# LSTM step with attention in a decoder: the first part's sum of exponentials on VectorE, the first alpha copy on ScalarE

## The reference

```python
def attend(h):
    q = h @ Wq.T
    scores = jnp.einsum('bc,bsc->bs', q, context)
    alpha = jax.nn.softmax(scores, axis=-1)
    ctx = jnp.einsum('bs,bsc->bc', alpha, context)
    return jnp.tanh(jnp.concatenate([ctx, h], axis=-1) @ Wout.T + b_out)

def step(carry, x_t):
    h, c, attn = carry
    gates = concat([x_t, attn]) @ W_ih.T + b_ih + h @ W_hh.T + b_hh
    i, f, g, o = jnp.split(gates, 4, axis=-1)
    c = sigmoid(f) * c + sigmoid(i) * tanh(g)
    h = sigmoid(o) * tanh(c)
    out = attn_out = attend(h)
    return ((h, c, attn_out), out)
```

## Time and profile before

| | us |
|---|---|
| median of 3 runs | 5888.53 (5887.12 to 5888.95) |
| profiled execution, its time | 5886.25 |
| profiled execution, its span | 5884.4 |
| PE busy in the span | 5294.2 (90%) |
| DVE busy | 3447.6 (59%) |
| ACT busy | 1998.7 (34%) |
| POOL busy | 352.6 (6%) |

### The profile page before, as it was taken

The page is one execution under the profiler, slowest core; times in us unless marked ns, Lnnn a source line. Parts: engine busy times, 40 slices in busy tenths (PEclk is TensorE's granted clock), DMA queues, the critical chain, the costliest instruction groups (busy, mean ns, idle before and its releaser), DMA issues. The chain is left out here.

```text
span 5884.4 us, 383798 instructions
## 1 busy us (share of the span) xinstructions
PE 5294.2 (90%) x171160; PEld 3829.2 (65%) x171160; DVE 3447.6 (59%) x15922; ACT 1998.7 (34%) x7989; POOL 352.6 (6%) x811
## 2 busy tenths in 40 slices
PE   6899999999999999999999999998887879797989
PEld 2477777777777777777777777776634334444433
DVE  4355555555555555555555555554588999999931
ACT  3143334333433333343334343433212122223221
POOL 0000000000000000000000000000111111112100
PEclk8999999999999999999999999999888889898999
DMA  1100000000000000000000000001211101010111
GB/s 71 59 2 2 2 2 2 2 2 2 2 2 2 2 2 2 2 2 2 2 2 2 2 2 2 2 2 42 79 45 40 42 24 50 29 50 29 50 39 54
DMA packets 45131, 111.57 MB, mean 19 GB/s; under 512 B 8160, under 2 KB 10208, under 8 KB 44528
## 3 DMA queue, kind: packets, MB, share of 16 engines
q1 hardware_dynamic: 43600, 109.39, 6.1%
q10 hardware_dynamic: 1440, 1.06, 0.1%
HBM read 99.90 MB, written 10.52 MB: 19 GB/s over the span
## 5 line engine op out<-in xcount | busy, mean ns | idle before, releaser
L712 PE MATMUL lstm_part_ps<-lstm_keys,lstm_hid 128*4 128x128 f32 x32768 | 1024.3, 273 | 205.7 <-DVE lstm_hid L881 205.7
L728 PE MATMUL lstm_ctx_ps<-lstm_values,lstm_alpha 128*4 128x128 f32 (+1 forms) x49152 | 1051.0, 237 | 0.0
L712 PEld LDWEIGHTS lstm_part_ps<-lstm_keys,lstm_hid 128*4 128x4 f32 x32768 | 770.2, 86 | 429.2 <-DVE lstm_hid L881 414.9
L728 PEld LDWEIGHTS lstm_ctx_ps<-lstm_values,lstm_alpha 128*4 128x4 f32 x49152 | 902.7, 86 | 91.5
L910 DVE TENSOR_REDUCE lstm_neg_max<-lstm_part_ps 128x1 f32<-128x128 f32 x1024 | 299.0, 292 | 678.1 <-PE lstm_part_ps L712 678.1
L844 ACT ACTIVATE lstm_expo<-lstm_part_ps,lstm_neg_max 128x128 f32<-128x128 f32 x1024 | 376.9, 368 | 861.6 <-DVE lstm_neg_max L910 861.6
L863 DVE STREAM_TRANSPOSE lstm_gates<-lstm_half_ps 128x96 f32<-128x96 f32 x1026 | 290.0, 283 | 597.7 <-PE lstm_half_ps L671 573.6
L671 PE MATMUL lstm_half_ps<-lstm_w_hid,lstm_hid 128*13 128x96 f32 x16384 | 600.8, 245 | 0.0
L671 PE MATMUL lstm_half_ps<-lstm_w_attn,lstm_attn 128*13 128x96 f32 x16448 | 447.9, 246 | 0.0
L671 PEld LDWEIGHTS lstm_half_ps<-lstm_w_hid,lstm_hid 128*13 128x13 f32 x16384 | 379.8, 93 | 0.0
L1944 ACT ACTIVATE mix_gated<-mix_gate_ps 115x512 f32<-115x512 f32 (+2 forms) x200 | 112.6, 563 | 774.9 <-PE mix_gate_ps L1672 774.8
(11 more groups left out here) (325 smaller groups left out, 8378.6 us busy)
## 6 DMA issues: line engine op xcount, KB each, us to landing
mix_ring<-in_sm_chunks SPq DMA_DIRECT2D x120, 358.0 KB, 3.0
mix_ring<-in_mix_chunks SPq DMA_DIRECT2D x80, 384.0 KB, 3.1
lstm_xg<-xg_rows SPq DMA_DIRECT2D x514, 16.0 KB
xg_rows<-lstm_xg_tile SPq DMA_DIRECT2D x16, 512.0 KB, 2.6
ctxT<-in_ctxT SPq DMA_DIRECT2D x1, 2048.0 KB, 14.3
out_xT<-xT SPq DMA_DIRECT2D x4, 512.0 KB, 3.8
xT<-in_xT SPq DMA_DIRECT2D x1, 1536.0 KB, 9.3
lstm_w_x<-in_lstm_w_x SPq DMA_DIRECT2D x1, 1024.0 KB, 10.3
```

What stands on the lines that cost most here:

```text
L712: mm = pe.matmul(part_rows(score_ps[part], b), hid[:, k, lo:lo + SPACE], keys[:, k, b * SRC + c * P:b * SRC + (c + 1) * P], start=(n == 0 ...
L728: mm = pe.matmul(part_rows(ctx_ps[n], b), alpha[:, b, c, SPACE - 1 - c:2 * SPACE - 1 - c], values[:, b * SC + c, ctx_cols[n]], start=(c == ...
```

## The change

It does three things in the LSTM step. The first part's exponential no longer has an accumulator: `exp_ready` is now raised by the exponential itself, and VectorE sums `expo[:, 0, :]` with a reduction of its own, raising the new `first_total_ready`. ScalarE instead of VectorE copies the first turned part to `alpha`, between its two exponentials. The second exponential keeps its accumulator. VectorE's copy of alpha 1 moves ahead of the spread of the totals. `alpha_ready` becomes one semaphore for each part.

```diff
@@ tensor
-                        pe.wait_ge(alpha_ready, 2 * t + 1)
+                        pe.wait_ge(alpha_ready[0], t + 1)
                         for n in range(PIECES):
                             context(0, n)
                         pe.wait_ge(exp_ready, 2 * t + 2)
                         turn(1)
                         for n in range(PIECES):
                             context(1, n)
-                        pe.wait_ge(alpha_ready, 2 * t + 2)
+                        pe.wait_ge(alpha_ready[1], t + 1)
@@ scalar
                         for part in range(PARTS):
                             act.wait_ge(max_ready, 2 * t + part + 1)
                             act.activation(expo[:, part, :], score_ps[part], ACT.Exp, bias=neg_max[:, part:part + 1],
-                                           accum_out=total[:, part:part + 1]).then_inc(exp_ready, 1)
+                                           accum_out=total[:, 1:PARTS] if part == 1 else None).then_inc(exp_ready, 1)
+                            if part == 0:
+                                act.wait_ge(alpha_turned, 2 * t + 1)
+                                act.copy(alpha_rows(0), turned_rows(0)).then_inc(alpha_ready[0], 1)
@@ vector
-                        keep_turned(t, 0)
                         dve.wait_ge(max_ready, 2 * t + 2)
                         dve.transpose(spread_blocks(spread_max[:, :]), every_row(neg_max[:, :])).then_inc(max_spread, 1)
                         dve.wait_ge(max_spread, t + 1)
                         dve.tensor_reduce(neg_max_all[:, :], spread_values(spread_max[:, :]), AX_XY, ALU.min)\
                            .then_inc(max_all_ready, 1)
+                        dve.wait_ge(exp_ready, 2 * t + 1)
+                        dve.tensor_reduce(total[:, 0:1], expo[:, 0, :], AX_X, ALU.add).then_inc(first_total_ready, 1)
+                        dve.wait_ge(alpha_turned, 2 * t + 2)
+                        dve.tensor_copy(alpha_rows(1), turned_rows(1)).then_inc(alpha_ready[1], 1)
+                        dve.wait_ge(first_total_ready, t + 1)
                         dve.wait_ge(exp_ready, 2 * t + 2)
                         dve.transpose(spread_blocks(spread_total[:, :]), every_row(total[:, :])).then_inc(total_spread, 1)
-                        keep_turned(t, 1)
                         dve.wait_ge(shrink_ready, t + 1)
```

More of the change, by code:

```diff
@@ L612, in attention_lstm_phase @@
             shrink_ready = q.sem("lstm_shrink_ready")
+            first_total_ready = q.sem("lstm_first_total_ready")
             total_spread = q.sem("lstm_total_spread")
@@ L619, in attention_lstm_phase @@
             alpha_turned = q.sem("lstm_alpha_turned")
-            alpha_ready = q.sem("lstm_alpha_ready")
+            alpha_ready = [q.sem(f"lstm_alpha{part}_ready") for part in range(PARTS)]
             ctx_ready = [q.sem(f"lstm_ctx{n}_ready") for n in range(PIECES)]
@@ L644, in by_part, with alpha_rows, turned_rows @@
                 return ap.rearrange("p (a c) -> p a c", a=PARTS)
+            def alpha_rows(part):
+                return alpha[:, :, 2 * part:2 * part + 2, SPACE - 1]
+            def turned_rows(part):
+                return turned_ps[part].rearrange("p (b r) -> p b r", r=2)
             @block.sync
@@ L882, in new_hidden @@
                                              in1=tanh_c[:, k, :], op0=ALU.add, op1=ALU.mult).then_inc(h_ready[k], 1)
[L884 to L887, removed]
                 for ps in (*half_ps, *part_ps, *ctx_bank):
```

## The result

| | before | after |
|---|---|---|
| median | 5888.53 us | 5857.91 us (5 runs, 5854.18 to 5859.06) |
| ratio | | 0.9947, 95% interval 0.9933 to 0.9960 |
| profiled span | 5884.4 us | 5856.1 us |

The account below looks back on a forecast made before the run. The LSTM loop, 7.46 us a step, was taken as bounded by the chain through TensorE's waits to `select(0)`. With `sel_ready` last, it loads 0.04 us earlier; times 512 is 20.5 us, so 5888.53 becomes 5868 us, range 5856 to 5891.

Parts of the forecast that it names:

- Read-out of the first exponential: First exponential without accumulator: 193 ns read-out goes, exponential stays 368 ns, first turn loads 0.09 us earlier.
- Alpha copy on ScalarE: First alpha copy, between the exponentials: takes 0.17 us, context load 0.09 earlier, second exponential not moved.
- Second alpha copy 0.09 earlier, by TensorE's queue: Second alpha copy on VectorE: starts at 2.23, 0.09 us earlier; TensorE's queue, not the second exponential, decides.
- VectorE's sum costs nothing: New reduction on VectorE: about 286 ns, ends at least 0.12 us before the second alpha copy, so free.
- Spread of the totals behind the copy: weighing 0.27 later, `sel_ready` last: VectorE after the second alpha copy: weighing 0.27 us later, `sel_ready` becomes `select(0)`'s last wait, load only 0.04 earlier.
- Behind it ... tanh and the next gates all move with `select(0)`.: After `select(0)` loads: `select(1)`, tanh and next gates shift equally, by the same 0.04 us a step.
- my own case: Whole step: gain of 0.03 to 0.06 us a step, 5858 to 5874 us; chance 0.62.
- the eaten gain: Rival, around the second alpha copy: extra wait cost or slower ScalarE copy leaves no change, 5878 to 5892; chance 0.21.
- ScalarE as the bound: Rival, ScalarE's copy ahead of exponential 1: exponential 0.12 late, step 0.06 us longer, 5919 us; chance 0.12.
- The full 0.09: Rival, whole step: all 0.09 us comes through, 46 us, 5842, needing a shorter `sel_ready` branch; chance past 0.06: 0.05.

Follow-up runs that it names:

- e3: Changed kernel with the first exponential's accumulator kept and VectorE's sum left out; 5899.35 us, ratio 1.0021.
- e2: Changed kernel with the first alpha copy back on VectorE, behind the second maximum; 5859.9 us, ratio 0.9951.
- e7: Changed kernel with one unused sum more on VectorE, ahead of the real one; 5862.4 us, ratio 0.9948.
- e1: Changed kernel with VectorE's spread of the totals moved ahead of its second alpha copy again; 5843.2 us, ratio 0.9925.
- e10: Changed kernel with two pairs of VectorE waits swapped, ahead of the weighing and of `sel_scaled`; 5843.4 us, ratio 0.9921.
- e8: Changed kernel with two unused sums more on VectorE, ahead of the real one; 5921.7 us, ratio 1.0049.
- e6: Changed kernel with TensorE's two waits ahead of `select(0)` swapped; 5903.6 us, ratio 1.0022.
- e9: e1 with TensorE's eight hidden-gate weight loads ahead of `select(0)` moved behind it; 5928.8 us, ratio 1.0069.
- e4: e1 with TensorE's two waits ahead of `select(0)` swapped; 5807.8 us, ratio 0.9866.
- e5: Kernel before the change, with only TensorE's two waits ahead of `select(0)` swapped; 5857.8 us, ratio 0.9939.

## Why the prediction was right, and where its size was off

- **Read-out of the first exponential.** Right: 367 ns without accumulator (368 taken), first turn loads at 0.42 (forecast 0.93 - 0.51 = 0.42), the wait 0.23. e3 shows that all the gain rests on it.
- **Alpha copy on ScalarE.** Right: 0.17 long, second exponential 0.88 behind the first, context load 0.96. What I did not say is that the copy could have stayed on VectorE at almost no cost (e2).
- **Second alpha copy 0.09 earlier, by TensorE's queue.** Right: 1.72, though the second turn's load moved by only 0.05 to 0.06, to the 1.38 at which its exponential was ready in my working (1.89 - 0.51). e3, with the second exponential 0.04 late, has it at 1.81, as before the change.
- **VectorE's sum costs nothing.** Right: 276 ns (forecast 286), and e7 has room for a second one.
- **Spread of the totals behind the copy: weighing 0.27 later, `sel_ready` last.** Right, and the step that decides how much of the 0.09 is left: `sel_scaled` ends 0.25 to 0.27 later (medians, rows; forecast 0.27), `select(0)` loads 0.046 earlier (forecast 0.04). e1 and e10 each lift it and reach 5843. I had said that this wait would appear in the list of waits; it does not, since TensorE idles only 0.11 there (loads end at 5.93 + 0.17 = 6.10, next 6.21). e8, with 0.16, has the row.
- **"Behind it ... tanh and the next gates all move with `select(0)`."** This is the term that was mis-sized. The second tanh moved by 0.066, not by 0.046: 0.020 a step, 10 us, because the wait met last now sits on the load. e6 shows it with nothing else changed, e9 without the hidden-gate loads ahead. e4 and e5 also have the last wait on the load, but their second tanh is 0.75 behind it; there the first tanh comes later (0.421 behind the load) and the second closer to it, and the load starts right behind TensorE's earlier loads (in e4's step those end at 3.45 + 0.17 = 3.62, and it starts at 3.63). Their loads follow each other as closely as in the changed kernel (0.007 from the first to the second), but the first matmul of `select(0)` starts 0.045 behind its load, against 0.002 in the changed kernel and 0.031 before. Whether the earlier matmuls hold it up, and what in TensorE makes the 0.02 with a separate instruction, stays open.

In sum, for the loop: 0.046 x 512 = 23.5 us at `select(0)`, 10.2 us behind it, less a remainder of 1.4 us, is 32.3 us. The forecast counted 20.5: 3 us of the difference lie in the 0.046 that I had as 0.04, most of the rest arose behind the load. That the median of 5857.9 still fell in the range is in part luck. It lies 2 us above the range's lower end and at the very edge of my own case (5858 to 5874), and the loop's gain alone would have given about 5856 (5888.5 - 32.3); the 4 us that came back outside the loop stood in no term of mine.

The rivals: the eaten gain needed up to 0.03 more for the spread's two waits behind the second copy, or a ScalarE copy of 0.21. The spread started 0.08 behind that copy as counted (1.721, 1.804), and ScalarE's copy took 0.17. ScalarE as the bound did not happen: the copy overlaps the exponential behind it (3.89 + 0.17 = 4.06, next start 4.03). Two figures of that rival were off without effect: the overlap in the earlier trace rows is 5.80 - 5.69 = 0.11, and by my own terms the gain is gone once exponential 1 starts at 1.44, not 1.46 (1.44 + 0.27 + 0.19 + 0.05 + 0.32 = 2.27, 0.04 behind the 2.23 of my case). The full 0.09 did not come through either; the loop gained 0.063 a step, past the 0.06 to which I gave a chance of 0.05, but by the wait on the load and not by a shorter `sel_ready` branch, which is what that rival needed.

## What to carry to other kernels

When an edit speeds up one branch of a join, work out the other branch to the same hundredth: here it took half of the 0.09. Then look at which wait of the join comes last and where it sits; after a change of order it is often another one. Of two waits ahead of one instruction, write first the one that is met last, so that it is the instruction's own. On TensorE's `select(0)` that one line was worth 33 us in the kernel before and 35 us on top of e1, and the wrong order cost 46 us in the changed kernel; in two places on VectorE it was worth 15 us (e10).

## What the runs showed of the hardware beyond what I expected

- A wait met last on a separate semaphore instruction costs, from the end of the producer: TensorE 0.11 to 0.12 us (before, e1, e6, e9), on the load itself 0.05 (after, e4, e5); VectorE 0.10 to 0.12 (after), on the instruction itself 0.04 (e10).
- On TensorE it also makes the first dependent result 0.02 us later (0.393 against 0.373 from first load to tanh), but for e4 and e5, where the load starts right behind others and the tanh 0.42 behind it. For `select(0)` the timeline marks the order: `x5` and `x3` where the wait is separate (before, e1, e6, e9, e10), `x8` in one row where it is not.
- The reduction of 128x128 from SBUF takes 276 ns (after) and a further one behind it only 0.19 us (e7, e8); ScalarE's copy of 128x8 from PSUM takes 0.17, the same as VectorE's (after).
